# Softmax attention in a hybrid layer: the probabilities are turned by VectorE and device memory instead of by TensorE

## The chip, the cores and the metric

The kernel runs on one core of one Trainium2 chip. The metric is the device time of one execution in microseconds (us); the median of three runs is compared. The engines are named as in the profile: PE is TensorE, DVE is VectorE, ACT is ScalarE, POOL is GpSimd, and SP is SyncE, which here only issues DMAs.

## The reference

The layer has four parts, each added to x: a chunked linear attention (A), a quantised gated FFN (F1), a softmax attention with one head of 512 columns (B), and the same FFN again (F2). The change touches B only. The tokens form two batches of 1024, and there are 512 columns:

```python
scale = 1.0 / jnp.sqrt(D)
Q = x @ W_q; K = x @ W_k; V = x @ W_v
scores = jnp.einsum('bqe,bke->bqk', Q, K) * scale
attn = jax.nn.softmax(scores, axis=-1)
out = jnp.einsum('bqk,bke->bqe', attn, V)
return jnp.einsum('bse,ed->bsd', out, W_o)
```

## The kernel before

Everything is in the SBUF of one core, and each engine runs an order written out by hand, with semaphores between the engines. Every fp32 operand is split into a high and a low fp16 part, and a product is three matmuls (high by high, high by low, low by high). `W_q W_k^T` and `W_v W_o` are multiplied out beforehand, so that B needs only a query product, a value product, the scores and the weighted sum.

Stage B handles one batch b after the other. A batch has eight rows of 128 queries (i = 0 to 7), taken as four pairs (p = 0 to 3). The steps on PE are:

- `query(b, s, n)`: four products of 12 matmuls for pairs 0 and 1 (s = 0), four for pairs 2 and 3 (s = 1). ACT (`a_copy`, `a_highs`, `s_high`), DVE and POOL (`query_parts`) drain and split them. They use PSUM banks 0 and 1 in turn, so product 2 can start only when `a_copy` has drained product 0.
- `values(i)`: eight products of 12 matmuls, also in banks 0 and 1, split by `v_high` (ACT) and `v_low` (DVE).
- `score(piece, p)`: the scores of a pair by a Strassen-like scheme in seven pieces of 6 matmuls. Pieces 1, 6, 7, 4 add up in bank 4. Between them ACT copies each partial sum out (`part_sum`) into `probs[0]` or `probs[1]`, 128 x 1024 fp32 each, one for the even row and one for the odd row of a pair. Pieces 2, 5, 3 use bank 5, and DVE adds them (`part_add`).
- Softmax of a row: DVE `row_max`, then ACT `softmax` (exponential with the row's sum).
- `turn_probs(i)`: eight PE transposes of 128 x 128 fp32 against the identity, into two PSUM banks. Then `pT_high` (ACT) and `pT_low` (DVE) split the turned row out of PSUM into fp16 tiles `pT`.
- `attend(i, t0, t1)`: 24 matmuls of the turned row with the split values, and `out_add(i)` (DVE) divides by the row's sum and adds to x.

While B works on batch 0 it also prepares batch 1's x, and while it works on batch 1 it prepares the next FFN block's x. `x_stats` and `x_normalise` (DVE) and `x_rstd` (POOL) make two normalised rows in `xn`; `turn_both(i)` transposes a pair of them on PE, with half 0 in bank 0 and half 1 in bank 1; `x_copy` and `x_row_highs` (ACT), `x_second` (DVE) and POOL take the banks apart. Bank 0 comes free with `x_copy`, bank 1 with `x_second`.

Three other sets of x rows, in the FFN stages, already go the way that the change now gives the probabilities. DVE transposes 32 x 32 blocks in place (`x_blocks`), SP writes the tile to device memory by four DMAs of 128 KB in pieces of 128 bytes (`blocks_to_dram`), waits for them, and reads it back by four more with the blocks in turned places (`blocks_to_turned`). All of SP's DMAs are issued in order.

ACT, DVE and POOL take their instructions strictly in the order written, so that an instruction that waits holds up all behind it on its engine.

Of the kernel before, what the change touches and what calls it, by code (L numbers as in the profile page):

```python
# [45 lines left out]

X_STATS = {(0, 2): ((0,), (1,), (2, 3)), (0, 3): ((4,), (5,), (6, 7))}
# [24 lines left out]
def ffn_uses(**more):  # L72
    uses = {0: 24, 1: 20, 2: 13, 3: 12, 4: 10, 5: 2, 6: 2, 7: 2}
    for name, n in more.items():
# [10 lines left out]
          ("B", 0, {0: 13, 1: 13, 2: 8, 4: 16, 5: 12, 6: 5, 7: 5}),  # L85
          ("B", 1, {0: 10, 1: 10, 2: 7, 4: 17, 5: 12, 6: 4, 7: 4}),
# [28 lines left out]
def hybrid_layer_kernel(nc, x, wq, wk, wv, w_ab, bq, bk, bv, b_ab,  # L115
# [3 lines left out]
    def at(name, offset, cols, dtype=F32):  # L119
# [18 lines left out]
           for v in range(2)]  # L138
# [76 lines left out]
               (Z + 112896, Z + 114944, Z + 116992), (Z + 86016, Z + 88064, Z + 90112))  # L215
# [57 lines left out]
    turned_lo = [at(f"turned_lo{b}", (Z + 47104, Z + 8192)[b], BTOK, F16) for b in range(2)]  # L273

# [5 lines left out]
    blocks = nc.dram_tensor("blocks", [4 * len(MOVED), QUADS, 2 * KT, P, SQ], F32, kind="Internal").ap()  # L280

# [117 lines left out]
    row_a_done = sem("row_a_done")  # L399
    row_b_done = sem("row_b_done")  # L400
# [179 lines left out]
    def pT(b, i):  # L580

        if i < 3:
            return tuple(t[b][:, :].rearrange("p (g n) -> p g n", g=2) for t in (turned_hi, turned_lo))
        if (b, i) in ((1, BT - 1), (1, BT - 2)):
            c = BTOK * (BT - 1 - i)
            return tuple(t[:, c:c + BTOK].rearrange("p (g n) -> p g n", g=2) for t in (s_hi, s_lo))
        return tuple(t[b][:, :].rearrange("p (k n) -> p k n", k=KT)[:, 0:2, GROUP:BTOK] for t in (xb_hi, xb_lo))
# [88 lines left out]
    with block as blk:  # L676

        @blk.sync
        def _(sp):
# [126 lines left out]

            weights_out()
            for q in MOVED:
# [6 lines left out]
                if q == B0:  # L815
                    weights_back()
            store(0, *range(BT))
# [6 lines left out]
        def _(pool):  # L824
# [212 lines left out]
            def pairs_of(q):  # L1037
                for i in range(4):
                    if (q, i) == (B1, 3):
                        x_ab_low(q, i)  # L1040
                        x_sums(q, i)
                    else:
                        x_sums(q, i)
                        x_ab_low(q, i)
                    x_12_low(q, i)

# [4 lines left out]
            query_parts(1, 0)  # L1051
            x_rstd(F2, *range(8))
            pool.wait_ge(x_34_lo, 4 * B1 + 4)
            for dst, src, less in ((3, 7, 1), (4, 2, 0), (5, 3, 1)):
                nc.gpsimd.tensor_tensor(cols(w_s, dst, HID), cols(w_gu, src, HID), cols(w_s, less, HID),
                                        ALU.subtract).then_inc(ws_ready, 1)
            query_parts(1, 1)
            pairs_of(F2)
            ffn("F2", 0)
# [4 lines left out]
        def _(act):  # L1064
# [335 lines left out]
            for b in range(BATCHES):  # L1400
# [6 lines left out]
                def part_sum(piece, p):  # L1407
# [3 lines left out]
                    row, half = {1: (0, 0), 6: (0, 1), 7: (1, 1), 4: (1, 0)}[piece]  # L1411
                    nc.scalar.activation(cols(probs[row], half), bank(4), ACT.Copy).then_inc(drained[4], 1)  # L1412
# [7 lines left out]
                def pT_high(i):  # L1420
                    use = turn_use(b, i)
                    u.full(use)
                    nc.scalar.activation(pT(b, i)[0], bank(use[0], 2).rearrange("p (g n) -> p g n", g=2), ACT.Copy,  # L1423
                                         scale=PS).then_inc(pT_hi_done, 1)

# [9 lines left out]
                for i in range(1, 6):  # L1435
                    v_high(i)
                part_sum(1, 0)
                part_sum(6, 0)
                part_sum(7, 0)
                v_high(6)  # L1440
                part_sum(4, 0)
                softmax(0)
                v_high(7)
                for p in range(4):
                    if (b, p) == (1, 3):
                        softmax(7)
                    pT_high(2 * p)
# [1293 lines left out]
```

## Time and profile before

| | |
|---|---|
| median of 3 runs | 946.29 us (945.65 to 947.17) |
| the profiled execution, its own time | 945.55 us |
| its span in the profile | 943.8 us |
| PE busy (matmul) | 930.4 us, 99% of the span |
| DVE, ACT, POOL busy | 608.2, 445.3, 425.9 us |
| chain that ended last | PE 93%, DVE 2%, ACT 1%, POOL 1%, DMA 1% |
| granted TensorE clock | full in all 40 slices |

The span is what the profiler's records cover, 1.8 us less than the execution's own time. The chain that ended last is followed back from the last instruction, each step to what released it; its share for PE says how much of the time was matmuls one behind another. PE busy counts overlapping matmuls once, so that a busy engine is not always at its peak.

### The profile page before, as it was taken

To read this page: it belongs to the slowest core of one execution; us is meant where nothing else is said; L and a number is where in the kernel's file an instruction comes from. 1 tells how busy PE (TensorE), PEld (TensorE's weight loads), DVE (VectorE), ACT (ScalarE), POOL (GpSimd) and SP (SyncE) were. 2 spreads that over 40 slices of the span, in tenths; PEclk is the share of its full clock that TensorE was granted. 3 is DMA by queue.
4 is the path that set the end of the run, shared out by engine and by line. 5 is a ranking of instruction groups with operands and counts; after the bars stand their busy time and mean duration, and the time that the engine had idled before them with its cause. 6 is when DMAs were issued, how large, how long until landed. Compare 5 with 4: busy or idle time off the path is not lost.

```text
span 943.8 us, 13107 instructions
## 1 busy us (share of the span) xinstructions
PE 930.4 (99%) x4654; PEld 525.6 (56%) x4670; DVE 608.2 (64%) x1148; ACT 445.3 (47%) x884; POOL 425.9 (45%) x447
## 2 busy tenths in 40 slices
PE   7999999999999999999999999999999999999998
PEld 4888988888734444444444455444455444444444
DVE  7555656949777777767655466446466777766643
ACT  4443334356577634663333354323455686246620
POOL 5433424377357654665630043304333466545530
PEclk9999999999999999999999999999999999999999
DMA  9501300024211190015500000000000001910001
GB/s 314 181 11 34 134 23 23 1 91 135 68 66 45 23 157 1 1 23 81 107 14 1 1 1 1 1 1 1 1 1 1 1 1 23 186 59 1 1 34 56
DMA packets 115008, 44.97 MB, mean 48 GB/s; under 512 B 101952, under 2 KB 102272, under 8 KB 114688
## 3 DMA queue, kind: packets, MB, share of 16 engines
q1 hardware_dynamic: 114944, 44.13, 18.1%
q8 instruction: 38, 0.62, 0.3%
q14 instruction: 26, 0.21, 0.1%
HBM read 32.56 MB, written 11.57 MB: 47 GB/s over the span
## 4 chain that ended last, share of the span: by engine, by line
PE 93%; DVE 2%; ACT 1%; POOL 1%; DMA 1%; SPq 1%; issue 1%; DVEq 0%; POOLq 0%
PE psum L2211 54%; PE psum L2458 14%; PE psum L2460 13%; PE psum L2608 7%; PE psum L2619 1%; DMA bq_col<-bq 1%; PE psum L2260 1%; PE psum L2345 1%; PE psum L2249 1%; ACT probs L1417 0%; DVE xb_lo L2116 0%; ACT xb_hi L1423 0%; DVE ln_bn L1532 0%; POOL wvT_lo L1007 0%; SPq L686 0%
## 5 line engine op out<-in xcount | busy, mean ns | idle before, releaser
L972 POOL TENSOR_TENSOR hid<-hid,hid_hi 128x512 f32<-128x512 f32 x88 | 102.9, 1170 | 110.1 <-DVE hid_hi L1888 110.1
L2458 PE MATMUL psum<-xf,w_gu 128*128 128x512 f16 x352 | 133.8, 380 | 0.1
L2458 PE MATMUL psum<-xf,w_s 128*128 128x512 f16 x264 | 100.1, 379 | 1.5 <-DVE up L1861 1.3
L2460 PE MATMUL psum<-xf,w_gu 128*128 128x512 f16 x264 | 100.0, 379 | 0.0
L2211 PE MATMUL psum<-wd_low,hid_lo 128*128 128x512 bf16 (+1 forms) x330 | 73.8, 373 | 0.2
L1286 ACT ACTIVATE hid_lo<-hid 128x512 f16<-128x512 f32 x88 | 54.9, 624 | 33.3 <-POOL hid L972 33.3
L968 POOL TENSOR_TENSOR hid<-up,gate 128x512 f32<-128x512 f32 x44 | 56.1, 1274 | 25.2 <-ACT gate L1281 25.2
L2460 PE MATMUL psum<-xq,w_s 128*128 128x512 f16 x176 | 66.7, 379 | 0.0
L2458 PEld LDWEIGHTS psum<-xf,w_gu 128*128 128x128 f16 x352 | 34.3, 97 | 54.6 <-ACT acc L1271 15.5
L1281 ACT ACTIVATE gate<-gate,sg_xs 128x512 f32<-128x512 f32 x44 | 31.7, 721 | 58.4 <-DVE gate L1871 58.4
L2211 PEld LDWEIGHTS psum<-wd_low,hid_lo 128*128 128x128 f16 x330 | 32.3, 98 | 36.8
L834 POOL TENSOR_TENSOR xrstd<-xvar,minus_half 128x1 f32<-128x1 f32 x48 | 25.5, 551 | 59.2 <-DVE xvar L1536 59.2
L1853 DVE TENSOR_TENSOR gate<-psum,acc 128x512 f32<-128x512 f32 x44 | 30.4, 692 | 31.1 <-ACT acc L1259 23.5
L1888 DVE TENSOR_SCALAR hid_hi<-hid 128x512 f16<-128x512 f32 x88 | 39.1, 444 | 16.1 <-POOL hid L968 14.6
L2211 PE MATMUL psum<-wd_b,hid_hi 128*128 128x512 bf16 (+1 forms) x190 | 45.8, 372 | 0.2
L2458 PEld LDWEIGHTS psum<-xf,w_s 128*128 128x128 f16 x264 | 25.9, 98 | 35.8 <-issue 4.9
L1871 DVE TENSOR_TENSOR gate<-psum,acc 128x512 f32<-128x512 f32 x44 | 30.4, 690 | 20.4 <-PE psum L2460 20.0
L2460 PEld LDWEIGHTS psum<-xf,w_gu 128*128 128x128 f16 x264 | 25.8, 98 | 30.8
L1412 ACT ACTIVATE probs<-psum 128x512 f32<-128x512 f32 x32 | 19.1, 597 | 48.3 <-PE psum L2608 48.3
L1880 DVE SCALAR_TENSOR_TENSOR hid<-psum,su_c,gate 128x512 f32<-128x512 f32 x44 | 33.0, 750 | 12.5 <-PE psum L2460 12.5
L1970 DVE TENSOR_TENSOR yt<-psum,sd_rows 128x512 f32<-128x512 f32 x31 | 21.1, 687 | 28.7 <-PE psum L2211 27.7
L1861 DVE SCALAR_TENSOR_TENSOR up<-psum,su_c,acc 128x512 f32<-128x512 f32 x44 | 33.0, 749 | 9.1 <-POOL hid L968 7.6
(336 smaller groups left out, 2430.8 us busy)
## 6 DMA issues: line engine op xcount, KB each, us to landing
turned<-blocks SPq DMA_DIRECT2D x36, 128.0 KB, 3.0
cla_wide<-cla_dram SPq DMA_DIRECT2D x16, 256.0 KB, 3.3
out<-xres SPq DMA_DIRECT2D x15, 256.0 KB, 2.0
xres<-x SPq DMA_DIRECT2D x3, 1024.0 KB, 13.0
blocks<-xn SPq DMA_DIRECT2D x24, 128.0 KB, 3.1
codes_gu<-gateT SPq DMA_DIRECT2D x1, 2816.0 KB, 11.5
codes_gu<-upT SPq DMA_DIRECT2D x1, 2816.0 KB, 10.6
codes_da<-downT SPq DMA_DIRECT2D x1, 1536.0 KB, 6.7
```

Source lines behind the costliest of these rows:

```text
L968: nc.gpsimd.tensor_tensor(hid2[:, :], up2[:, :], gate2[:, :], ALU.mult).then_inc(hid2_done, 1)
L972: nc.gpsimd.tensor_tensor(hid[:, :], hid[:, :], hid_part(hid_hi, j, half), ALU.subtract).then_inc(rest_done, 1)
L1281: nc.scalar.activation(gate2[:, :], gate2[:, :], ACT.Silu, scale=sg_xs[:, j:j + 1]).then_inc(silu2_done, 1)
L1286: nc.scalar.activation(hid_part(hid_lo, j, half), hid[:, :], ACT.Copy, scale=LO).then_inc(lo_done, 1)
L1853: nc.vector.tensor_tensor(cols(gate1, j % 2), bank(2), acc1[:, :], ALU.add).then_inc(drained[2], 1)
L1861: nc.vector.scalar_tensor_tensor(out=up2[:, :], in0=bank(3 + j % 2), scalar=su_c[:, j:j + 1], in1=acc3[:, :], op0=ALU.mult, op1=ALU.add).t ...
L1880: nc.vector.scalar_tensor_tensor(out=hid1[:, :], in0=bank(j % 2), scalar=su_c[:, j:j + 1], in1=cols(gate1, j % 2), op0=ALU.mult, op1=ALU.m ...
L1888: nc.vector.tensor_scalar(hid_part(hid_hi, j, half), hid[:, :], ROUND, -ROUND, ALU.add, ALU.add).then_inc(hi_done, 1)
L2211: return nc.tensor.matmul(out, lhsT, rhs, start=start, stop=stop)
L2458: nc.tensor.matmul(bank(use[0]), w, x_operand(piece, k, False), start=start and k == 0, stop=False, skip_group_check=not start)
L2460: last = nc.tensor.matmul(bank(use[0]), w, x_operand(piece, k, True), start=False, stop=k == 1, skip_group_check=not start)
L2608: last = nc.tensor.matmul(bank(use[0]), l, r, start=start and k == 0 and j == 0, stop=k == 1 and j == 2, skip_group_check=not start)
```

## The change

Row i of the probabilities is no longer transposed on PE. DVE transposes its 32 x 32 blocks in place in `probs[i % 2]` (`p_blocks`), SP writes it to `prob_blocks` in device memory by four DMAs, waits, and reads it back turned into the same buffer by four DMAs (`probs_turned`). ACT and DVE then split the row from SBUF (`pT_high`, `pT_low`). Because the row stays in its buffer until `pT_low`, `part_sum` of the next pair waits for that. The even rows' `pT` have new tiles of their own.

The PSUM banks 2 and 3 that the transposes used go to score pieces 5 and 3, each by itself; for piece 3 DVE adds both banks, one addition more for each pair. The order changes on every engine: on PE a pair's pieces run as `first_row` (1, 2, 6, 5, 3), then an `attend`, then `second_row` (7, 4); the first score pieces run before the last value products (`VALUES_FIRST`); `turn_both(2p-2)` and `turn_both(2p-1)` both lie in pair p; on POOL the sums of FFN weights move in two parts. The core of the diff:

```diff
+VALUES_FIRST = (3, 1)
+    even_hi = at("even_hi", Z + 110080, BTOK, F16)
+    even_lo = at("even_lo", Z + 112128, BTOK, F16)
+    prob_blocks = nc.dram_tensor("prob_blocks", [BATCHES * BT, QUADS, BT, P, SQ], F32, kind="Internal").ap()
     def score_use(piece, p):
         return {1: (4, 4 * p), 6: (4, 4 * p + 1), 7: (4, 4 * p + 2), 4: (4, 4 * p + 3),
-                2: (5, 3 * p), 5: (5, 3 * p + 1), 3: (5, 3 * p + 2)}[piece]
-    def turn_use(b, i):
-        return (4, 16) if (b, i) == (1, BT - 1) else (2, i)
+                2: (5, p), 5: (2, p), 3: (3, p)}[piece]
+    def probs_free(b, i):
+        return b * BT + i - 1
@@ SP
+            def probs_turned(b, i):
+                n, t = b * BT + i, probs[i % 2]
+                sp.wait_ge(p_blocks_done, n + 1)
+                src = t[:, :].rearrange("p (m j) -> p m j", j=SQ)
+                for a in range(QUADS):
+                    sp.dma_start(prob_blocks[n, a].rearrange("m (c i) j -> i (m c) j", c=QUADS),
+                                 src[a * SQ:(a + 1) * SQ, :, :]).then_inc(p_out[i % 2], 16)
+                sp.wait_ge(p_out[i % 2], p_all(b, i))
+                dst = t[:, :].rearrange("p (m a j) -> p m a j", a=QUADS, j=SQ)
+                for a in range(QUADS):
+                    sp.dma_start(dst[:, :, a, :],
+                                 prob_blocks[n, a].rearrange("m p j -> p m j")).then_inc(p_moved[i % 2], 16)
@@ POOL
             query_parts(1, 0)
+            pool.wait_ge(x_34_lo, 4 * B1 + 4)
+            weight_sums((4, 2, 0), (5, 3, 1))
             x_rstd(F2, *range(8))
--            pool.wait_ge(x_34_lo, 4 * B1 + 4)
-            for dst, src, less in ((3, 7, 1), (4, 2, 0), (5, 3, 1)):
...
             query_parts(1, 1)
             pairs_of(F2)
+            Use(pool, "B", 1).full(out_use(1, 4))
+            weight_sums((2, 6, 0), (3, 7, 1))
@@ ACT
                 def part_sum(piece, p):
+                    if probs_free(b, 2 * p + row) > 0:
+                        act.wait_ge(pT_lo_done, probs_free(b, 2 * p + row))
                 def pT_high(i):
-                    use = turn_use(b, i)
-                    u.full(use)
+                    act.wait_ge(p_moved[i % 2], p_all(b, i))
+                    if i > 1:
+                        u.full(out_use(b, i - 2))
@@ ACT, the loop over the pairs as it is now
                 for p in range(4):
                     if p < 3:
                         part_sum(1, p + 1)
                         part_sum(6, p + 1)
                     if p == 2:
                         x_12_high(q, 1)
                     if p == 3:
                         x_12_high(q, 3)
                     pT_high(2 * p + 1)
                     if p < 3:
                         softmax(2 * p + 2)
                     if p == 2:
                         x_34_high(q, 1)
                     if p == 3:
                         x_34_high(q, 3)
                     if p < 3:
                         part_sum(7, p + 1)
                         part_sum(4, p + 1)
                         softmax(2 * p + 3)
                         pT_high(2 * p + 2)
                     if p == 0:
                         parts_high(b, 1)        # a_copy, a_copy, then a_highs and s_high twice
                     if p in (1, 2):
                         x_copy(q, 2 * p - 2)
                         x_highs(q, 2 * p - 2)
                         x_34_high(q, 2 * p - 2)
                         x_copy(q, 2 * p - 1)
                         x_row_highs(q, 2 * p - 1)
                     if p == 3 and b == 0:
                         parts_high(1, 0)
@@ DVE
+                    if piece == 3:
+                        u.full(score_use(5, p))
+                        nc.vector.tensor_tensor(x, bank(score_use(5, p)[0]), x, ALU.add).then_inc(half_done, 1)
+                        dve.wait_ge(half_done, 4 * b + p + 1)
+                    nc.vector.tensor_tensor(x, bank(use[0]), x, ALU.add).then_inc(drained[use[0]], 1)
+                def p_blocks(i):
+                    dve.wait_ge(probs_done, b * 8 + (i + 1))
+                    nc.vector.transpose(probs[i % 2][:, :], probs[i % 2][:, :]).then_inc(p_blocks_done, 1)
@@ DVE, the loop over the pairs as it is now
                 for p in range(4):
                     if p < 3:
                         part_add(2, p + 1)
                         part_add(3, p + 1)
                         row_max(2 * p + 2)
                     pT_low(2 * p + 1)
                     if p < 3:
                         p_blocks(2 * p + 2)
                     if p == 2:
                         x_34_low(q, 1)
                     if p == 3:
                         x_34_low(q, 3)
                     if p == 0:
                         for l in range(4, 8):
                             x_stats(q, l)
                     if p == 1:
                         x_normalise(q, 0)
                     out_add(2 * p)
                     if p < 3:
                         part_add(5, p + 1)
                         row_max(2 * p + 3)
                     if p in (1, 2):
                         x_turned(q, 2 * p - 2)
                         x_normalise(q, 2 * p - 1)
                     if p < 3:
                         p_blocks(2 * p + 3)
                         pT_low(2 * p + 2)
                     if p == 0:
                         query_parts(b, 1, 0)
                         query_parts(b, 1, 1)
                     if p in (1, 2):
                         x_second(q, 2 * p - 2)
                         x_34_low(q, 2 * p - 2)
                         x_second(q, 2 * p - 1)
                     if p == 1:
                         x_normalise(q, 2)
                     if p == 3 and b == 0:
                         query_parts(1, 0, 0)
                         query_parts(1, 0, 1)
                     out_add(2 * p + 1)
@@ PE
-                def turn_probs(i):
...
-                        u.read_out(turn_use(b, i))
+                        pe.wait_ge(pT_lo_done, b * 8 + i + 1)
@@ PE, the order of a batch as it is now
+                for i in range(VALUES_FIRST[b]):
+                    values(i)
+                first_row(0)
+                for i in range(VALUES_FIRST[b], 6):
+                    values(i)
+                second_row(0)
                 values(6)
                 values(7)
                 for p in range(4):
+                    if p < 3:
+                        first_row(p + 1)
+                    attend(2 * p)
+                    if p < 3:
+                        second_row(p + 1)
+                    if p == 0:
                         for n in range(4):
                             query(b, 1, n)
                     elif p < 3:
+                        turn_both(2 * p - 2)
                     elif b == 0:
+                        for n in range(4):
+                            query(1, 0, n)
+                    attend(2 * p + 1, 0, 6)
+                    if p in (1, 2):
+                        turn_both(2 * p - 1)
+                    attend(2 * p + 1, 6, 8)
```

## Rows read from the trace of the kernel before

**Rows 1.** Windows, stage B: us, busy of each engine, PEclk, DMA share, GB/s

```profile
468.30:729.30 261.00, 260.63 (x1298) 128.98 (x1297) 148.32 (x267) 107.23 (x170) 76.89 (x76) 1.00 0.01 5
```

**Rows 2.** Chain that ended last: start us, us, what ran

```profile
494.41 6.47 PE psum L2608 x30
508.66 0.94 PE psum L2619 x8
517.51 0.87 PE psum L2619 x8
553.86 0.87 PE psum L2260 x8
```

**Rows 3.** Timeline of PE: the matmul behind score piece 1, and the first of F2

```profile
495.55 0.38 PE L2608 MATMUL psum<-xb_hi,a_hi 128*128 128x512 f16 x1
729.12 0.38 PE L2458 MATMUL psum<-xf,w_gu 128*128 128x512 f16 x1
```

**Rows 4.** Timeline of ACT in stage B, idle time before it in brackets

```profile
495.75 0.60 ACT L1412 ACTIVATE probs<-psum 128x512 f32<-128x512 f32 x1 [0.70 <-PE psum L2608]
507.11 1.24 ACT L1417 ACTIVATE probs<-probs,nmax,mids 128x1024 f32<-128x1024 f32 x1 [0.41 <-DVE nmax L2110]
508.26 0.19 ACT L1417 ACTIVATION_READ_ACCUMULATOR probs<-probs,nmax,mids 128x1 f32 x1
509.63 1.02 ACT L1423 ACTIVATE turned_hi<-psum 128x1024 f16<-128x1024 f32 x1 [0.34 <-PE psum L2619]
554.39 0.59 ACT L1081 ACTIVATE x_first<-psum 128x512 f32<-128x512 f32 x1
```

**Rows 5.** Timeline of DVE in stage B

```profile
504.81 0.69 DVE L2098 TENSOR_TENSOR probs<-psum,probs 128x512 f32<-128x512 f32 x1
505.61 1.22 DVE L2108 TENSOR_REDUCE smax<-probs 128x1 f32<-128x1024 f32 x1
510.69 1.23 DVE L2116 SCALAR_TENSOR_TENSOR turned_lo<-psum,turned_hi 128x1024 f16<-128x1024 f32 x1 [0.67 <-ACT turned_hi L1423]
512.83 0.69 DVE L1532 BATCH_NORM_STATS2 ln_bn<-xres 128x6 f32<-128x512 f32 x1
516.85 0.20 DVE L2124 TENSOR_SCALAR mids<-rowsum,mids 128x1 f32<-128x1 f32 x1
556.36 0.68 DVE L1582 TENSOR_TENSOR xb_lo<-psum,xb_hi 128x512 f16<-128x512 f32 x1
```

**Rows 6.** Source view, DVE transposes: duration ns min/median/max, first and last start

```profile
L1559 DVE STREAM_TRANSPOSE xn<-xn x6: 1233/1240/1246, 310.4 to 805.0; 128x1024 f32<-128x1024 f32 x6
```

**Rows 7.** Source view, DMAs out, 305 to 325 us, a tile alone

```profile
L763 SPq DMA_DIRECT2D blocks<-xn x4: 343/590/620, 311.7 to 313.3; - x4
DMA to landing us min/median/max: 2.1/2.6/4.2
```

**Rows 8.** Timeline, FFN stages: a tile's issues, and who waited for it

```profile
450.76 2.93 SPq L782 DMA_DIRECT2D turned<-blocks  x4
455.83 0.63 ACT L1092 ACTIVATE xb_hi<-turned 128x512 f16<-128x512 f32 x1 [1.65 <-DMA turned<-blocks]
801.84 2.23 SPq L763 DMA_DIRECT2D blocks<-yt  x4
804.17 3.43 SPq L782 DMA_DIRECT2D turned<-blocks  x4
807.03 1.29 DVE L1970 TENSOR_TENSOR yt<-psum,sd_rows 128x512 f32<-128x512 f32 x2 [0.78 <-DMA blocks<-yt]
809.91 0.42 ACT L1092 ACTIVATE xf<-turned 128x256 f16<-128x256 f32 x1 [4.56 <-DMA turned<-blocks]
```

**Rows 9.** Windows, while such tiles move without a pause

```profile
437.00:457.00 20.00, 19.89 (x93) 9.10 (x93) 15.59 (x23) 6.60 (x11) 10.28 (x9) 1.00 1.08 166
```

**Rows 10.** Groups by line, stage B, POOL: count, busy us, mean ns

```profile
L1055 POOL TENSOR_TENSOR w_s<-w_gu,w_s 128x1408 f16<-128x1408 f16 x3 | 8.5, 2855 | 0.0
```

**Rows 11.** Timeline of PE at the start of the span

```profile
4.07 4.34 PE L2211 MATMUL psum<-mask_b,ident_b 128*128 128x512 bf16 x10 [4.07 <-POOL mask_b L875]
```

More of the change, by code:

```diff
@@ L816, in _ @@
                     weights_back()
+                    for b in range(BATCHES):
+                        for i in range(BT):
+                            probs_turned(b, i)
             store(0, *range(BT))
@@ L1038, in pairs_of, with weight_sums @@
                 for i in range(4):
[L1039 to L1044, printed above, removed]
+                    x_sums(q, i)
+                    x_ab_low(q, i)
                     x_12_low(q, i)
+            def weight_sums(*which):
+                for dst, src, less in which:
+                    nc.gpsimd.tensor_tensor(cols(w_s, dst, HID), cols(w_gu, src, HID), cols(w_s, less, HID),
+                                            ALU.subtract).then_inc(ws_ready, 1)
             query_parts(0, 0)
@@ L1420, in pT_high, with parts_high @@
                 def pT_high(i):
-                    use = turn_use(b, i)
-                    u.full(use)
-                    nc.scalar.activation(pT(b, i)[0], bank(use[0], 2).rearrange("p (g n) -> p g n", g=2), ACT.Copy,
+                    act.wait_ge(p_moved[i % 2], p_all(b, i))
+                    if i > 1:
+                        u.full(out_use(b, i - 2))
+                    nc.scalar.activation(pT(b, i)[0], probs[i % 2][:, :].rearrange("p (g n) -> p g n", g=2), ACT.Copy,
                                          scale=PS).then_inc(pT_hi_done, 1)
+                def parts_high(*which):
+                    a_copy(*which, 0)
+                    a_copy(*which, 1)
+                    for c in range(2):
+                        a_highs(*which, c)
+                        s_high(*which, c)
                 if b == 0:
@@ L1434, in _ @@
                     s_high(0, 0, 1)
-                for i in range(1, 6):
+                for i in range(1, VALUES_FIRST[b]):
                     v_high(i)
@@ L1476, in _ @@
+                    if p == 2:
+                        x_34_high(q, 1)
+                    if p == 3:
+                        x_34_high(q, 3)
+                    if p < 3:
+                        part_sum(7, p + 1)
+                        part_sum(4, p + 1)
+                        softmax(2 * p + 3)
+                        pT_high(2 * p + 2)
+                    if p == 0:
+                        parts_high(b, 1)
                     if p in (1, 2):
@@ L1583, in x_second, with x_turned @@
                                         x_2(q, i, 0), ALU.subtract).then_inc(done, 1)
+            def x_turned(q, i):
+                phase, b, one, two = x_banks(q, i)
+                Use(dve, phase, b).full(two)
             def x_34_low(q, i):
@@ L2591, in score @@
                     use, n = score_use(piece, p), q_n(b, p // 2, 1)
-                    start = piece in (1, 2, 5)
+                    start = piece in (1, 2, 5, 3)
                     if piece == 1:
@@ L2610, in score @@
                     last.then_inc(filled[use[0]], 1)
-                def turn_probs(i):
-                    use = turn_use(b, i)
-                    pe.wait_ge(probs_done, b * 8 + (i + 1))
-                    u.free(use)
-                    if use[0] == 4:
-                        u.free((5, 12))
-                    for t in range(BT):
-                        last = nc.tensor.transpose(bank(use[0], 2)[:, t * P:(t + 1) * P],
-                                                   probs[i % 2][:, t * P:(t + 1) * P], ident[:, :])
-                    last.then_inc(filled[use[0]], 1)
                 def attend(i, t0=0, t1=BT):
@@ L2644, in turn_both, with first_row, second_row @@
                     turn_x(q, i, 1)
+                def first_row(p):
+                    for piece in (1, 2, 6, 5, 3):
+                        score(piece, p)
+                def second_row(p):
+                    score(7, p)
+                    score(4, p)
                 if b == 0:
```

230 lines of the change are left out of this document (80 added, 150 removed).

## The prediction, made before the changed kernel was run

> **What bounds the kernel now.** I read the page's chain first: 93% of it is PE. The windows view of stage B says the same of the only stage that changes: 260.63 of 261.0 us busy on PE, 148 on DVE, 107 on ACT, DMA 1%, clock full [rows 1]. The stage begins at 468.3 us, and the first matmul of F2 is at 729.1 [rows 3]. So in B only what PE runs, or waits for, counts; the others have room, but as chains of waits, not as sums.
>
> PE's own work follows from the chain [rows 2]: 30 score matmuls in 6.47 us, 0.216 each. So a piece (6) is 1.295 us, a query or value product (12) 2.59, an `attend` (24) 5.18. Eight transposes of a row of probabilities take 0.87 to 0.94 us, a `turn_both` (8) 0.87. Without `turn_probs` the stage holds 32 products (82.9), 56 pieces (72.5), 16 attends (82.9) and 8 pairs (7.0): 245.3 us. The 16 turns are 16 x 0.9 = 14.4 us, and 261 - 245.3 - 14.4 leaves about 1.1 us of small pauses.
>
> **What is removed.** 14.4 us of PE, all on the path. That is the whole possible gain, with 1.1 us more if the pauses went too.
>
> **The price of one turn now.** Block transpose on DVE: 1.24 us for 128x1024 [rows 6]. Then SP: the x tiles of the FFN stages have the same bytes (512 KB in four DMAs) and the same 128-byte pieces, so their rows serve directly.
> - Out leg, alone: the fourth issue starts 1.6 us after the first and lands at least 2.1 us later, 3.7 [rows 7]. With another tile in flight DVE waited for it from 801.84 to 807.03, 5.2 [rows 8].
> - Back leg: first issue to the reader's start 5.1 (450.76 to 455.83) and 5.7 (804.17 to 809.91) [rows 8].
>
> The round trip R (including 0.1 us at SP's wait) is thus 8.9 to 11.0 us. I take 9.4: 3.8 out, since SP is otherwise idle in B, and 5.5 back. It is the sum of two legs because SP waits between them. Even data movement alone would need 0.524 MB / 166 GB/s = 3.2 us a leg [rows 9].
>
> The Trainium skill (DMA: Bandwidth & Descriptors, Anatomy of one DMA) gives a DMA a fixed cost of about 2.0 us, mostly the write receipt, for the path from GpSimd. An estimate by it would be 1.6 + 2.0 + 0.3 = 3.9 us a leg, R = 7.9, and some 9 us less in the total below; the trace's back legs, 5.1 and 5.7, don't agree.
>
> **What a buffer then goes through.** Steps, with prices: PE to ACT or DVE 0.20 (495.55 to 495.75) [rows 3, 4]; `part_sum` 0.60, `softmax` 1.24 + 0.19, `pT_high` 1.02 [rows 4]; `part_add` 0.69, `row_max` up to the exponential's start 1.5 (505.61 to 507.11), `pT_low` 1.23 [rows 4, 5]. From SBUF instead of PSUM I take `pT_high` and `pT_low` as unchanged (less by up to 0.3 each is possible).
>
> (a) Score piece 4 now follows 7 at once, in the same bank, with ACT's copy between: 0.20 + 0.60 + 0.05 (a release between engines, as 510.65 to 510.69) = 0.85 us of pause, eight times. Before, other work lay between them. Six of the eight lie in stretches that are paced by something longer (b, c); two, ahead of each batch's loop, count: 1.7.
>
> (b) Pair p = 0. Time F is the start of `first_row(1)`. Row 1's blocks are ready at F + 1.2 (behind `v_low(6)`), back at F + 10.6. `pT_high(1)` is ahead of `softmax(2)` on ACT, so row 2 starts its own trip only then: pT_high to F + 11.7, softmax to 13.1, blocks to 14.4, back at 23.9. ACT's next instructions are `softmax(3)` (ready at 23.2, behind four row statistics of 1.0 each and `out_add(0)` on DVE [rows 5]), `pT_high(2)` to 24.9, and only then `a_copy`, to 25.5. PE has run first_row(1), attend(0), second_row(1) and two queries by F + 20.8 and needs bank 0 for the third: it waits 4.8 us. Two queries and attend(1) more: F + 35.9. PE's work there is 29.8 (7 pieces 9.06, 4 queries 10.36, 2 attends 10.36), so 6.1 us are lost, 12.2 in both batches. Behind the wait everything of PE is queued; nothing can pass it.
>
> (c) Pairs p = 1 and 2. Time S is the start of `first_row(p+1)`. Its last piece ends at S + 6.5; two adds to 8.1; row_max to 9.7; softmax to 11.1; blocks to 12.4; trip to 21.9; pT_high to 22.9. Only behind it does ACT run `x_copy` of pair 2p-2, and only behind `pT_low` (24.1) DVE its `x_second`. Before, from x_copy's start to the end of x_second took 2.7 us (554.39 to 557.04) [rows 4, 5], so bank 1 is free at 25.6. PE is there much earlier: pieces 6.5, attend 5.2, 7 and 4 with their pause 3.4, turn_both 0.9, six eighths of an attend 3.9 make S + 19.9. It waits for bank 0 until 23.6, turns half 0, waits for bank 1 until 25.7, turns half 1, and runs the last quarter of the attend: S + 27.4. PE's work is 21.2. 6.2 us are lost, four times: 24.8.
>
> (d) Pair p = 3 has no scores. Row 7's trip waits for SP to issue row 6's back leg (S + 20), so `pT_low(7)` of pair 2's count ends at about S + 31.9 and attend(7) starts at S + 32.6 in batch 1: nothing lost, cover 0.7 us. In batch 0 the queries lie between.
>
> **Covered at nothing.** The first row of each batch: batch 0's row 0 is back 8 us before attend(0). DVE's 16 transposes (19.8 us) and 8 more adds (5.5) fit in its 113 idle us; what of them lies on a chain is in (b) and (c). SP: 2 x 7 us of issue and wait in 27. POOL's two last weight sums (2 x 2.86 [rows 10]) end some 3 us ahead of F2's first use; if that cover went, up to 3 us. The other half of them, the new tiles and banks cost nothing. A wait of `part_sum(1, 1)` on `pT_low(0)` costs 0.5 us of pause and is inside F + 20.8.
>
> **The sum.** 1.7 + 12.2 + 24.8 = 38.7 us of new pauses, less 14.4 and 1.1: +23.2. On the profiled execution's 945.55 us (span 943.8 and 1.8 around it) that is 968.8; the median of the runs is 0.7 higher. I predict 969.
>
> **Range.** R stands twice in (b) per batch and once in each (c): eight times when it grows, about six when it shrinks, since softmax(3) then takes over. R = 8.9: -3; R = 11.0: +13. Steps shorter by 0.3 in SBUF: -5 at most. Together with the next case's upper part: 957 to 984.
>
> **Rivals.**
> 1. *The trips are hidden after all.* Then only (a) is left, all eight: 945.55 - 15.5 + 6.8 = 936.9. For it: SP and the DMA engines are idle in B [rows 1], and the wanted row is always one attend ahead. Against: (c) stays PE-paced only if its chain shrinks by 5.4 us, R of 4.0, less than the 6.4 that the bytes take. It decides for the gain only if I misread the order, so that x_copy and x_second don't stand behind the split. The point from which it is faster: pauses below 15.5 us in all, less than half of mine. Chance 5%.
> 2. *The clock falls in the pauses.* At the span's start, after 4.07 us without work, ten matmuls of 512 columns took 4.34 us [rows 11], about 0.44 apart, which is the 1.2 GHz level, though the granted clock reads full. Six pauses of 3.7 to 4.8 us come; if each cost the same again, ten slow matmuls with 0.22 lost in each, that is 2.2 us, 13 in all: 982. Against: every later pause in the trace is shorter, so nothing shows a fall. Chance 12%. The Trainium skill (TensorE: Matmul & The Clock Gate, the HAM clock gate) has a rule by which an idle engine goes back to half rate; no row behind the start shows it.
> 3. *Half the trip.* The legs run shorter than the FFN stages', for want of traffic (R near 7): (c) becomes 25.0, (b) 33.7, the total 955. The rows of a lone out leg are already in my value. Chance 10%.
> 4. *The change does not do what it says*, that is the time is the same because some pauses of before vanish: there are only 1.1 us of them. Chance 2%.
>
> My case has 71%, 962 to 980. Slower by over 0.2% (1.9 us, about what a measurement can tell) 93%, within 2%, faster 5%.
>
> **What would show it.** Right: PE busy in B falls by about 14 us while the stage grows to some 284; PE's waits name DVE `x_mid`/`xb_lo` (x_second) or ACT `x_first` in p = 1 and 2, and ACT `a_f` (a_copy) before the third query of each batch; ACT's waits name DMA probs; SP's issues of a row lie about 4 us apart, out to back. (a) shows as pauses of 0.85 between pieces 7 and 4, named ACT probs. Wrong: round trips below 8 us, the loop of (c) off 27.4 by more than 2, matmuls 0.43 us apart behind a pause, or waits for POOL.

## The result, and the profile after

The changed kernel takes 986.0 us (median of 4 runs) where the kernel before takes 946.4 on the same chip: ratio 1.042, 95% interval 1.0398 to 1.0441. It is 39.6 us slower. I had forecast 969 us, 22.7 slower, with 984 as the end of the range. The sign and the place were right, and the size was too small by 17.

| us | before | after |
|---|---|---|
| profiled execution | 945.6 | 986.0 |
| its span | 943.8 | 984.2 |
| stage B, first matmul to F2's first | 260.8 | 299.4 |
| stages before B / from F2 on | 468.3 / 214.7 | 469.7 / 215.1 |
| mean granted clock | 1.0 | 0.982 |

Stage B holds 38.6 of the 40.4 us by which the span grew. Windows of the kernel after, the whole stage and then stretches of 5 us in it; the columns are those of [rows 1]:

```profile
469.70:769.10 299.40, 262.21 (x1169) 118.85 (x1167) 175.81 (x291) 109.00 (x171) 82.57 (x77) 0.94 0.37 60
533.00:538.00 5.00, 0.96 (x3) 0.44 (x4) 2.47 (x2) 2.33 (x5) 1.02 (x1) 0.86 1.02 164
538.00:543.00 5.00, 5.00 (x20) 2.02 (x19) 0.98 (x2) 0.90 (x2) 0.93 (x2) 0.79 0.59 93
573.00:578.00 5.00, 2.61 (x10) 1.85 (x11) 2.66 (x5) 3.44 (x6) 2.19 (x3) 0.62 0.64 99
688.00:693.00 5.00, 5.00 (x13) 1.71 (x12) 0.46 (x1) 0.18 (x1) 1.05 (x1) 0.50 0.75 122
728.00:733.00 5.00, 5.00 (x17) 1.99 (x16) 3.67 (x6) 2.04 (x5) 3.84 (x5) 0.68 0.44 69
```

Two things stand here. PE is now idle for 37.2 us of the stage, where it was idle for 0.4. And its busy time did not fall by the 14.4 us of the turns that went: it rose, from 260.6 [rows 1] to 262.2, though it issues 129 matmul records fewer. The reason is the column before the last two, the granted clock: 0.94 over the stage, and 0.50 to 0.79 in the stretches behind its long pauses. From 688 to 693 PE is busy all the time and gets 13 matmuls done where 23 fit at full clock.

What PE waited for in stage B (in total, times, longest):

```profile
PE psum L2296 <- ACT x_first L1113: 17.1, 4, 5.4
PE psum L2247 <- ACT a_f L1411: 9.5, 2, 5.5
PE psum L2644 <- ACT probs L1446: 6.2, 8, 0.8
PE psum L2296 <- DVE xb_lo L1604: 2.2, 2, 1.1
PE psum L2296 <- DVE xq L1604: 2.1, 2, 1.3
```

These are the waits of the prediction by name and count: `x_copy` four times, `a_copy` twice, `part_sum` eight times, `x_second` four times (the last two lines); 37.1 us in all. One of them, before the third query of batch 0, in PE's timeline (five more rows of the same spacing left out), then in ScalarE's:

```profile
531.21 0.38 PE L2247 MATMUL psum<-xb_hi,g_lo 128*128 128x512 f16 x1
537.04 0.59 PE L2247 MATMUL psum<-xb_hi,g_hi 128*128 128x512 f16 x1 [5.45 <-ACT a_f L1411]
537.42 0.63 PE L2247 MATMUL psum<-xb_lo,g_hi 128*128 128x512 f16 x1
...
539.98 0.42 PE L2247 MATMUL psum<-xb_lo,g_hi 128*128 128x512 f16 x1
540.24 0.38 PE L2247 MATMUL psum<-xb_hi,g_lo 128*128 128x512 f16 x1
```
```profile
535.36 1.06 ACT L1458 ACTIVATE even_hi<-probs 128x1024 f16<-128x1024 f32 x1 [2.06 <-DMA probs<-prob_blocks]
536.32 1.07 ACT L1411 ACTIVATE a_f<-psum 128x512 f32<-128x512 f32 x2
```

`pT_high(2)` waits for the trip of row 2, `a_copy` runs right behind it, and PE resumes 0.7 us after `a_copy` starts. The matmuls behind the pause start about 0.43 us apart, seven of them, before they are back at 0.216. The chain that ended last says the same in one line; PE was 93% of it before:

```profile
PE 75%; DMA 7%; DVE 6%; SPq 5%; ACT 3%; issue 2%; POOL 2%; DVEq 0%; ACTq 0%; POOLq 0%
```

SP's issues of the trips of rows 2, 3 and 4 (L827 out, L832 back):

```profile
524.69 2.25 SPq L827 DMA_DIRECT2D prob_blocks<-probs  x4
530.59 2.43 SPq L832 DMA_DIRECT2D probs<-prob_blocks  x4
534.61 2.25 SPq L827 DMA_DIRECT2D prob_blocks<-probs  x4
539.36 2.31 SPq L832 DMA_DIRECT2D probs<-prob_blocks  x4
561.21 2.25 SPq L827 DMA_DIRECT2D prob_blocks<-probs  x4
567.68 2.43 SPq L832 DMA_DIRECT2D probs<-prob_blocks  x4
```

The outward legs, from first issue to first issue, are 5.90, 4.75 and 6.47 us long. Nine of the sixteen rows take 4.37 to 4.39, two more 4.60 and 4.75. The way back is 4.8 to 5.0 where ScalarE waits for it (530.59 to `pT_high` at 535.36, 567.68 to 572.63), but for row 0 with 5.9. So an undisturbed round trip is 4.4 + 5.0 = 9.4 us, and rows 2, 4, 5, 6 and 7 of batch 0 have outward legs of 5.5 to 6.5. Experiments 8 to 12 look for the cause of these long legs.

Stretch by stretch, from one `first_row` to the next (the last one to `attend(6)`):

| stretch | predicted | batch 0 | batch 1 |
|---|---|---|---|
| p = 0 | 35.9 | 38.05 | 37.96 |
| p = 1, 2 (each) | 27.4 | 31.05, 31.6 | 28.8, 29.1 |

The six together are 15.1 us over the prediction. Two suspects: the clock behind the pauses, and the long outward legs.

### The profile page after: what moved, and what is told of

It reads as the page before. It is cut to its first block, busy times and chain, and to the rows that moved or that the text cites. A ratio compares the mean times of both kernels' runs of the same rounds, so it can differ in the third digit from the quotient of the medians.

```text
span 984.2 us, 13032 instructions
## 1 busy us (share of the span) xinstructions
PE 932.4 (95%) x4526; PEld 515.4 (52%) x4542; DVE 635.3 (65%) x1172; ACT 447.2 (45%) x884; POOL 433.8 (44%) x448
## 4 chain that ended last, share of the span: by engine, by line
PE 75%; DMA 7%; DVE 6%; SPq 5%; ACT 3%; issue 2%; POOL 2%; DVEq 0%; ACTq 0%; POOLq 0%
PE psum L2247 43%; PE psum L2494 13%; PE psum L2496 12%; PE psum L2644 5%; DMA prob_blocks<-probs 3%; DMA probs<-prob_blocks 3%; SPq L832 1%; SPq L827 1%; DVE probs L2146 1%; DMA bq_col<-bq 1%; SPq L777 1%; ACT probs L1451 1%; PE psum L2296 1%; SPq L796 1%; DVE smax L2139 1%
## 5 line engine op out<-in xcount | busy, mean ns | idle before, releaser
L2247 PEld LDWEIGHTS psum<-wd_low,hid_lo 128*128 128x128 f16 x330 | 32.3, 98 | 36.8
L1915 DVE TENSOR_SCALAR hid_hi<-hid 128x512 f16<-128x512 f32 x88 | 39.1, 445 | 15.9 <-POOL hid L999 14.4
L875 POOL TENSOR_TENSOR x_last<-x_mid,x_first 128x256 f32<-128x256 f32 x12 | 8.8, 730 | 91.1 <-DVE x_mid L1602 91.0
```

The source lines that it names most:

```text
L1915: nc.vector.tensor_scalar(hid_part(hid_hi, j, half), hid[:, :], ROUND, -ROUND, ALU.add, ALU.add).then_inc(hi_done, 1)
L2247: return nc.tensor.matmul(out, lhsT, rhs, start=start, stop=stop)
```

## The experiments

**1. No trip.** SP's part goes; `pT_high` waits for the block turn alone. (This and the two other kernels "without the trip" below leave the exchange of 32-column blocks out.)

```
-  for b, i: probs_turned(b, i)                        # SP
-  act.wait_ge(p_moved[i % 2], p_all(b, i))            # in pT_high
+  act.wait_ge(p_blocks_done, b * BT + i + 1)
```

> The changed kernel without the trip through device memory: ACT's pT_high waits for the block transpose on DVE and splits the row as it is; SP's 128 DMAs are gone, so the weighted sum gets rows turned in blocks only. All else, DVE's transposes and every order included, is as in the changed kernel. Theory A (the trip's length in a chain of waits makes the loss): PE's waits for x_first and a_f go, only the 0.94 us between score pieces 7 and 4 stay, eight times 7.5 us, no pause is long enough for a slow stretch of PE; 986.0 - 17 - 9.5 - 4 (x_second) - 10 to 12 (clock) - about 3, 937 to 942 us, below the kernel before. Rival B (the work added on DVE and the new orders make the loss, whatever the trip): at most 10 us faster than the changed kernel, 976 or more.

Measured: 956.9 us (two runs), ratio 1.012 (1.0096 to 1.0137). The trips are worth 29 us, not the 44 to 49 that I expected by theory A, nor the 10 at most of rival B: even at no price for the round trip the changed order is 11 us slower than before. The three largest of PE's waits, two rows of ScalarE, and one window:

```profile
PE psum L2641 <- ACT probs L1443: 6.2, 8, 0.8
PE psum L2244 <- ACT a_f L1408: 4.0, 2, 2.0
PE psum L2293 <- DVE xb_lo L1601: 3.4, 2, 1.7
```
```profile
529.20 1.24 ACT L1448 ACTIVATE probs<-probs,nmax,mids 128x1024 f32<-128x1024 f32 x1 [3.64 <-DVE nmax L2138]
531.38 1.06 ACT L1408 ACTIVATE a_f<-psum 128x512 f32<-128x512 f32 x2
```
```profile
703.00:706.00 3.00, 3.00 (x9) 1.03 (x7) 0.96 (x1) 2.02 (x4) 2.85 (x3) 0.50 0.00 0
```

`a_copy` (531.38) still stands behind `softmax(3)`, for which ScalarE waits 3.64 us on VectorE's row maximum, and behind `pT_high(2)`, which now waits for nothing; `x_second` stands behind `pT_low`. I had taken it that all of this would vanish with the DMAs. The clock also fell to 0.50 three times: behind both waits of 1.99 us for `a_copy`, and behind two waits of 0.32 and 1.46 us, 2 us apart.

**2. The six long pauses filled.** 19 or 15 useless matmuls (4.1 or 3.2 us) where PE waits, into a free bank.

```
+  if n == 2: fill(p, 19, ...)      # before the third query
+  fill(p, 15, ...)                 # before turn_x(2p-1, 0)
```

> The changed kernel with matmuls of no use put into PE's six long pauses: 19 before the third query of each batch, 15 before each turn_both(2p-1), into bank 3 when its last use is read out. The trip and the orders stay. Theory C (the clock's fall after each pause costs a part of its own): the slow stretches (matmuls 0.43 us apart) go, pauses themselves stay; the two queries' 1.5 and 2.9 us, and 1.7 us plus 0.6 in each of four pairs, together 12 to 13 us less some chain-bound part: 974 to 978 us. Rival D (PE is only waiting for the chain, slow matmuls lie inside waits anyway): within 2 us of 986.

Measured: 976.3 us, 9.7 less than the changed kernel, within the expectation of the clock's theory. In the profiled execution the granted clock is full in all of stage B; the whole stage, and two of the stretches shown above:

```profile
469.00:756.30 287.30, 269.97 (x1268) 123.42 (x1266) 175.81 (x291) 108.09 (x170) 82.03 (x77) 1.00 0.38 63
538.00:543.00 5.00, 5.00 (x25) 2.25 (x23) 2.46 (x5) 2.75 (x5) 1.40 (x2) 1.00 0.67 105
573.00:578.00 5.00, 5.00 (x26) 2.51 (x27) 2.38 (x5) 2.72 (x5) 3.84 (x4) 1.00 0.67 105
```

Work that does nothing made the kernel faster, so the slow matmuls are not a by-product of the waiting itself. The 98 useless matmuls take 21.1 us of the 270.0; that leaves 248.9 of work, where the changed kernel is busy for 262.2: its slow matmuls add 13.3 us, 2.2 for each of the six falls. The median gives back 9.7 of them, 1.6 for each. It understates them: the profiled execution, 973.1 us, is the only one of the four with the clock at 1.000 to the end, and it is 12.9 below the changed kernel; the others took 974.7, 977.9 and 979.2 at mean clocks of 0.998, 0.995 and 0.995. The useless matmuls also move the long legs (rows 2, 4, 5, 8 and 10 now); experiments 11 and 12 repeat the comparison with nearly all of these out.

**3. Unhooked.** The copies for which PE waits are moved ahead of the instructions that wait for a trip, and most of them ahead of `softmax(2p+3)` too; the trips stay.

```
   # ACT, p (shortened)
   part_sum(7), part_sum(4)
+  a_copy(b, 1, 0); a_copy(b, 1, 1)       # p == 0
+  x_copy, x_row_highs(2p-2)              # p == 1, 2
   softmax(2p+3)
+  x_12_high(2p-2)                        # p == 1, 2
   pT_high(2p+2)
   # DVE, p == 1, 2
+  x_second(q, 2p-2)
   p_blocks(2p+3); pT_low(2p+2)
```

> The changed kernel with three groups of steps put ahead of the wait for the trip: on ACT a_copy (pair 0) and x_copy, x_row_highs, x_12_high of pair 2p-2 before pT_high(2p+2); on DVE x_second of pair 2p-2 before pT_low(2p+2). The trips stay. Theory A (it is the place in the queue behind the trip, not the trip, that PE pays for): the six long pauses go, and with them the slow clock; left are the 0.94 us of pieces 7 and 4 (7.5), about 1 us at the first pairs, and 0 to 4 us where batch 0's long out legs (6.5 us) make part_sum(1) late: 941 to 947 us. Rival B2 (the buffer probs is what waits for the trip: a row's full chain through the buffer is longer than PE's work in a pair): pauses move to part_sum(1), the time stays above 965.

Measured: 959.1 us, 27 less than the changed kernel, ratio 1.0144 (1.0127 to 1.016). All waits on `a_f`, `x_first` and the pairs are gone, which shows that the long pauses came from where these copies stood in the queues, as steps (b) and (c) said. But it is 12 to 18 us above what I expected, and below the 965 of rival B2, because the rows themselves are now what comes late (the three largest waits):

```profile
PE psum L2652 <- ACT probs L1446: 8.6, 9, 2.3
PE psum L2255 <- DVE xb_lo L2158: 3.9, 1, 3.9
PE psum L2255 <- DVE even_lo L2158: 3.5, 1, 3.5
```

**4. Unhooked, and pieces 7 and 4 kept apart.**

```
-  second_row(p + 1)                # 7, 4
+  attend(2p, 0, 6); score(7, p+1); attend(2p, 6, 8); score(4, p+1)
```

> As the unhooked kernel, and score pieces 7 and 4 no longer follow one another: the last quarter of attend(2p) lies between them (for the first pair a value product). Theory A: 8 x 0.94 us less, unless the chain through the buffer (about 22.2 us for 21.2 of PE work) is then the bound, which gives back up to 1 us in four pairs: 934 to 941 us, faster than both kernels. Rival B2: no gain over the unhooked kernel, as the buffer's chain sets the pace.

Measured: 961.0 us, 1.9 more than the kernel of experiment 3. The eight pauses behind piece 7 became four of up to 2.7 us, and the waits on the split rows grew. By the code the `part_sum` of a row waits for `pT_low` of the row two before it in the same buffer. I read the result as the buffer's way round setting the pace; no run here isolates that.

**5 and 6. The same two kernels without the trip.**

> The unhooked order (query and step copies ahead of the trip's drains) and no trip through device memory: the turned rows are read straight from the block-wise turned tile, so the output is not the reference's. With the two runs beside it this is the fourth corner of a square: changed kernel 986.0, without the trip 956.9, unhooked 959.1. Theory A (the trip costs only through the copies queued behind it, and through the rows that wait for it): the two edits took mostly different waits, as the trip-less kernel still had 2.2 us pauses at the queries and slow matmuls after them and the unhooked one had its waits at attend(6), attend(7) and part_sum; near-additive, 930 to 940. Theory B (what is left after either edit is the place of each row behind softmax and VectorE's order, the same in both): 945 to 955. Above 946.3 also means that the new order alone, without any trip, is no better than the kernel before.

> As the unhooked kernel without the trip, and pieces 7 and 4 of the scores kept apart by six attend steps; output not the reference's. With the trip this separation brought nothing (959.1 to 961.0), which I read as: the buffers' way round sets the pace there. Theory A: without the trip the buffers come free early, the eight pauses of 0.94 us between pieces 7 and 4 close for six of them, so 4 to 7 us less than the kernel beside it, 925 to 935. Theory B (the pauses only move to the next wait for the partial sums whatever the trip takes): within 1.5 us of the kernel beside it.

Measured: 941.8 us, ratio 0.9956 (0.9943 to 0.997), and 941.7. The kernel of experiment 5 closes a square:

| us | hooked | unhooked |
|---|---|---|
| with the trip | 986.0 | 959.1 |
| without | 956.9 | 941.8 |

```profile
468.30:726.00 257.70, 249.15 (x1175) 114.45 (x1174) 179.43 (x292) 108.09 (x171) 85.18 (x78) 1.00 0.02 5
```
```profile
PE psum L2649 <- ACT probs L1443: 6.2, 8, 0.8
```

The trip costs 29 us where the copies hang behind it and 17 where they don't; the two effects overlap by 12, so the run lies between theory A (930 to 940) and B (945 to 955), 1.8 us from A. Read the other way, moving the copies gains 27 us with the trip and 15 without any, so more than half of that gain does not need the trip: it comes from their place behind the softmax and the split. Without both, the change would be worth 4.0 us: 14.4 of turns gone, against 7.5 for eight pauses behind piece 7 (from the first matmul of 7 to that of 4 it is 2.23 us, 1.295 for the piece and 0.94 of pause, of which the view counts 0.78) and 2.3 for single waits on `pT_low`. Experiment 6 missed: keeping 7 and 4 apart bought nothing without the trip either. Its two remaining waits there are longer (2.6 each), so the pause only moves, and behind the first of them the clock is at 0.50 for about three us.

**7. Row 3 alone.** The kernel before, with row 3 of each batch sent through device memory. There the `part_sum`, the copies and four queries stand between its softmax and its attend.

```
+  p_blocks(3)                      # DVE, p == 1, ahead of query_parts
+  probs_turned(0); probs_turned(1) # SP, behind weights_back
-  turn_probs(3)                    # PE
```

> The kernel before, with only row 3 of each batch turned on VectorE and sent through device memory; all other rows turn on TensorE as before. There softmax(3) ends 31.6 us before attend(3) starts, TensorE has four query products between, VectorE is idle from 534.4 to 539.5 and nothing else waits at that place. Theory A (a trip costs nothing where rows of the trace show 10 us of other TensorE work between, and removes one turn of 0.87 us in each batch): 1.7 us less than before, 943.5 to 945.5, ratio 0.997 to 0.9995. Theory B (the copy of row 3 on ScalarE waits for the trip past the moment at which the part sums of row 4 are due, 547.8): 0 to 5 us more than before.

Measured: 944.7 us (11 runs) against 945.75 (15 runs), ratio 0.9987, interval 0.9978 to 0.9996. Small, but outside the uncertainty, in the direction of theory A, and the only complete kernel here that beats the one before. In ScalarE's timeline the row is split in its old place with no wait for the trip (before: 547.42), and PE has no new wait:

```profile
546.36 1.04 ACT L1446 ACTIVATE xb_hi<-probs 128x1024 f16<-128x1024 f32 x1
```

**8. Block buffers reversed**, to find the cause of the long outward legs.

```
-  prob_blocks[n, a]
+  prob_blocks[BATCHES * BT - 1 - n, a]
```

> The unhooked kernel with the order of the sixteen block buffers in device memory reversed, nothing else. In four kernels the outward leg of row 2 of the first batch took 5.86 to 5.90 us from first issue to the return's first issue, rows 4 to 7 of the first batch often 5.5 to 6.5, and the others 4.38. Theory A (the slow legs go with the place in device memory): rows 2, 4, 5, 6, 7 of the first batch now take 4.4 us and rows 13, 11, 10, 9, 8 of the sixteen 5.5 to 6.5. Theory B (they go with the moment in the program, whatever the address): the same rows of the first batch stay slow. Time within 1 us of the unhooked kernel's 959.1 in both.

Measured: 955.7 us (one run, 3.3 below experiment 3, where I expected at most 1 of difference; this is not explained), and the same rows are slow: 5.58, 6.40 and 6.11 for rows 2, 4 and 6 of batch 0, 4.37 and 4.38 for rows 8, 9 and 10. It is the moment, not the address. SP's row 2:

```profile
523.04 2.25 SPq L827 DMA_DIRECT2D prob_blocks<-probs  x4
528.62 2.41 SPq L832 DMA_DIRECT2D probs<-prob_blocks  x4
```

What is special about the moment stands in the DMA view. Row 4 of the changed kernel, 561.2 to 567.6 us, in 40 slices of 0.16 us, and its queue of kind "instruction":

```profile
DMA  0000039989999999999999200000000111000000
GB/s 0 0 0 0 0 66 201 190 158 202 213 214 182 195 214 214 195 197 305 200 194 163 27 0 0 0 0 0 0 0 2 7 8 10 12 12 0 0 0 0
q8 instruction: 1, 0.02, 1.9%
```

The 512 KB have moved by slice 23, 3.7 us after the first issue, at some 200 GB/s. Then nothing, and about 1.1 us later a trickle at 2 to 12 GB/s, after which SP's wait ends. In that leg lies one transfer of 16 KB on queue q8. The view calls its kind instruction; that it is TensorE's own code is what the next experiment tests.

**9. The code shifted.** The unhooked kernel with 64 useless matmuls of 32 columns early in stage B.

```
+  for _ in range(64): mm(bank(3)[:, 0:32], g_hi[:, 0:P], xb_hi[b][:, 0:32], True, True)
```

> The unhooked kernel with 64 useless matmuls of 32 columns after the first values product of batch 0, which move TensorE's instructions by half of the spacing (21 to 35 us) at which the trace shows transfers of queue q8 (kind: instruction, 16 KB). In five kernels, 80 outward legs, each leg over 5.1 us either holds such a transfer or starts at most 2.6 us after the return of the row before was issued; all others took 4.37 to 4.81 us. Theory A (the instruction transfer, a part of TensorE's own code, delays packets of the leg): the transfers fall elsewhere, rows 2, 4 and 6 of the first batch take 4.4 us, and whichever rows now hold one take 5.1 to 6.5. Theory B (something else of that moment, or the transfer only happens beside it): rows 2, 4 and 6 stay at 5.6 to 6.4 without a transfer in them. Time: 2 to 4 us above 959 for the added work, less up to 3 for legs that get shorter.

Measured: 953.8 us (two runs), 5.3 less than the unhooked kernel though 1.8 us of work was added. On the time I was wrong (958 to 963 expected); part of the gain is that the clock falls once in stage B where it fell twice. On the legs theory A holds. The q8 transfers that fell at 504, 525 and 559 us now fall at 491, 515 and 548, so matmuls added to TensorE's code move them. Rows 2, 4 and 6 take 4.39, 4.38 and 4.38, and row 1, which now holds a q8 transfer, 5.98. SP's row 2 (before the shift 5.89):

```profile
526.25 2.25 SPq L827 DMA_DIRECT2D prob_blocks<-probs  x4
530.64 2.76 SPq L832 DMA_DIRECT2D probs<-prob_blocks  x4
```

**10. Row 7 of batch 0 too**, on top of experiment 7, by the same edit at p = 3.

> The kernel with row 3 alone through device memory (944.7), and row 7 of batch 0 too. Before: softmax(7) ends 590.8 and attend(7) starts 604.1, with 15.5 us of queries and attend(6) between, less the turn that goes. The row needs 1.2 (turn of blocks) + 9.4 (trip) + 2.3 (both drains) = 12.9, so it would be ready at 603.7 where TensorE comes to it at 603.2. Theory A (such a row costs only what it lacks of cover): 0.3 to 0.9 us less than with row 3 alone, 943.5 to 944.6. Theory B (an outward leg with an instruction transfer, 1.1 to 2 us longer, or the clock after a short wait): 0 to 2 us more than with row 3 alone.

Measured: 948.6 us, 3.9 more than with row 3 alone, outside both theories, and slower than before (1.0012 to 1.003). The outward leg held a q8 transfer, 5.73 us. PE then waited 2.58 us for the row, and `attend(7)` ran at the lower clock, 6.88 us instead of 5.18:

```profile
605.65 0.39 PE L2255 MATMUL psum<-v_hi,xb_hi 128*128 128x512 f16 x1 [2.58 <-DVE xb_lo L2153]
```
```profile
606.00:609.00 3.00, 3.00 (x9) 1.06 (x7) 1.86 (x5) 1.85 (x3) 1.09 (x2) 0.50 0.00 0
```

2.6 + 1.7 less the turn's 0.9 is 3.4 of the 3.9. The fall of the clock shows from run to run: four of the eleven executions had the clock at 1.000 and took 946.7 to 947.0 us, the other seven had 0.998 and took 948.5 to 949.6. By my own numbers the row came 0.5 us too late even with clean legs; the long leg added 1.3 and the fall about 2.

**11 and 12. The shift in the changed kernel, and in the kernel of experiment 2.** The same line as in experiment 9.

> The changed kernel, nothing else than the 64 useless matmuls of 32 columns (1.8 us) that move TensorE's instruction transfers by half of their spacing. In the changed kernel rows 2, 4 and 6 of batch 0 hold one in their outward leg (5.90, 6.47, 6.48) and rows 5 and 7 start 2.5 us after the return before and take 5.5. Theory A (the part of the miss that is not the clock's is these legs: 1.5 + 2.1 + 1.1 + 2.1 + 1.1 = 7.9 us of legs, of which rows 2 to 6 are waited for): 978 to 983 with the added work in it. Theory B (the slow legs are mostly covered): 985 to 989.

> The changed kernel with its six long pauses filled with useless matmuls (976.3 that way) and with the same shift of TensorE's code. There rows 2, 4, 8 and 10 held a transfer. Theory A (prediction 968.8 plus nothing but the clock's part, taken out here, and the slow legs, mostly taken out here): 970 to 974 with 1.8 us of added work. Theory B (something third is in the miss): 975 to 979.

Measured: 982.4 and 971.5 us, both as theory A expected. In experiment 11 all sixteen outward legs take 4.37 to 4.68, though row 1's holds a q8 transfer; row 4, for instance:

```profile
560.64 2.25 SPq L827 DMA_DIRECT2D prob_blocks<-probs  x4
565.02 2.40 SPq L832 DMA_DIRECT2D probs<-prob_blocks  x4
```

With the 1.8 us of added work taken off, the long legs cost 986.0 - 982.4 + 1.8 = 5.4 us; the executions of either kernel lie 3 to 4 us apart, so this is rough. In experiment 12 both suspects are out, but for one leg of 6.05 on row 1: 971.5 - 1.8 = 969.7 us, 0.9 above the prediction's 968.8. Against experiment 11, with the code in the same place at the start of the stage, full clock is worth 10.9 us. Its p = 0 stretches are 36.8 and 35.0 (predicted 35.9), its loops 27.3, 27.0, 27.0 and 27.0 (27.4).

## Why the prediction was wrong

**What held.** The bound: only what PE runs or waits for counts. The gain of 14.4 us. The mechanism of (b) and (c), by name, count and order of the waits; experiment 3 shows it by taking the queueing away. Only, experiments 1 and 5 show that the trip is not the whole of what the copies queue behind. The round trip, 9.4 us, though put together differently: 4.4 out and 5.0 back where I had 3.8 and 5.5. `pT_high` from SBUF, 1.06 us where it was 1.02 from PSUM. (d): nothing lost. The covered items: in F2 PE waits for nothing, as before. Of (a), 0.94 us where I had 0.85. The 3.2 us a leg that I took from [rows 9] as what the bytes need is a mean over 20 us and no limit: in the leg shown above they moved in about 2.9 us. Only the refusal of rival 1 used it. The sum of these steps is within 1 us of the run that has neither of the two effects below.

**The step that failed** is the choice against rival 2, the clock, to which I gave 12%. My reason was that every later pause in the trace of before is shorter, "so nothing shows a fall". That is no evidence against one: the trace held no pause of that length except the one at the start [rows 11], and behind that one the matmuls were slow. The only relevant row spoke for the rival. The sum put the clock at nothing without evidence for that; it should have been a term. Its price was also right: 13 us for six falls, where the slow matmuls added 13.3 us of TensorE time, and full clock gave back 9.7 (experiment 2, medians) to 12.9 (its profiled execution), and 10.9 between experiments 11 and 12. The rule that I cited there from the Trainium skill (TensorE: Matmul & The Clock Gate, the HAM clock gate), an idle engine goes back to half rate, agrees with the granted clock of 0.50 at 688 to 693. The Trainium skill (the same page, HAM oscillation) describes a kernel in which each wait for a DMA is followed by slow matmuls; here it is a wait for a copy queued behind a DMA, with the clock at 0.50 behind each of the six.

**The term that was mis-sized** is the outward leg, 3.8 us "since SP is otherwise idle in B". SP was idle, but code transfers fall into some legs, and I had not counted them. A clean leg is 4.4, and five legs of batch 0 were 5.5 to 6.5: 5.4 us in all. I had read the rows of the FFN stages, 5.2 us [rows 8], as a leg with another tile in flight, and kept that price out of the sum.

Taken out one after the other, 5.4 for the legs (experiment 11) and 10.9 for the clock (experiment 12) make 16.3 of the 17.2 us missing; in the other order it is 9.7 and 6.6. The last 0.9 is not settled. In the profiled execution 1.4 us of the miss lie ahead of stage B, in stages that the change hardly touches; in that of experiment 12 it was 0.3.

**Not foreseen at all**: that the changed order costs 11 us against before even without any trip (experiment 1), as long as the copies stand behind the softmax and the split of the next rows; and that 17 us of the trip stay when nothing of TensorE's is queued behind it (experiments 3 and 5).

## What to carry to other kernels

An instruction that waits, for a transfer or for another engine, holds back everything queued behind it on its engine. Put what other engines need soon ahead of it, and only then price the transfer. When a forecast contains pauses of several microseconds on TensorE, add the slow matmuls behind each one: here 1.6 to 2.2 us per pause. In this kernel the trip of 9.4 us, with the block turn and the split (12.9 in all), belongs where at least 13 us of other TensorE work lie between the softmax and the first use, with a margin of 2 us, since a leg was longer by up to that.

## What the runs showed of the hardware that I had not expected

- **Code loading delays the end of data DMAs.** In eight kernels (the changed one and experiments 2, 3, 4, 8, 9, 11 and 12) there are 128 outward legs. 26 hold a transfer of q8 (16 KB, instructions): 22 of these took 5.1 to 6.5 us and four 4.4. Nine legs without one start at most 2.6 us after the issue of the return before and took 5.2 to 5.5. The other 93 took 4.37 to 4.81, median 4.39. The ways back say the same, where ScalarE waited for them: 66 without a q8 transfer took 4.6 to 5.3 us, and of 18 with one, ten took 5.4 to 6.2. Adding 64 matmuls moved the transfers and cleared the legs that had been long. Why some transfers did no harm is open: the four fell 3.5 us or more behind the first issue, but so did eight of those that did harm.
- **The clock falls sooner than the one pause of before suggests, and a pause's length alone does not tell.** It was granted at 0.50 behind a pause of 2.58 us (experiment 10), behind waits of 1.99, and behind waits of 0.32 and 1.46 us (experiment 1). It stayed full behind 2.33 us (experiment 3, at 569.96), behind 0.32 and 1.72 us (experiment 1, at 566.92), and behind eight pauses of 0.94 us (experiment 5).
- **Useless matmuls can pay twice**: filling the waits gave 9.7 us (medians), and displacing the code fetches 5.4.
